# A scan-based decoder layer on one core: softplus without the inverse exponential, logarithms in place, and most Silus of z moved into the scan stage

## The chip, the cores and the metric

One core of one Trainium2 chip runs the whole program. The metric is the device time of one execution in microseconds, as a median over runs. All data is float32 in HBM.

## The reference, cut to what matters

Four sequences of 512 tokens of width 512 go through three residual blocks, each behind a layer norm. The change touches the first (a selective state-space block) and the order of work around the others: a SmoothQuant int8 feed-forward (its output is the "second residual") and a mixture of 16 experts, two per token, with a shared expert.

```python
xz = einsum(in_proj_weight, hidden)          # 512 -> 2048, halves x and z, 1024 channels each
x = silu(conv1d(x))                          # depthwise, 4 taps
dt, Bc, Cc = split(x_proj(x))                # 128, 16, 16
delta = softplus(dt_proj_weight @ dt + dt_proj_bias)
h = h * exp(delta * A) + (delta * u) * B     # 16 states per channel, one step per token
y = sum_n(h * C) + u * D
y = y * silu(z)
out = out_proj_weight @ y
```

Softplus is computed as relu(x) + ln(w) less a correction, with e = exp(-|x|) and w = 1 + e rounded. The correction makes good what the rounding of w lost: lost = (w - 1) - e, times 1/w.

## The kernel before, in words

**Tiling.** Channels lie in 8 blocks of 128 partitions, tokens (512) along the free axis. A batch's stage is 128 units (8 blocks times 16 states), p = 0 to 127 with a tail of 8. Per unit ScalarE makes exp(delta * A) (`decay`, line 942, into a ring of three PSUM banks), VectorE runs the scan over tokens (line 1277) and multiplies by C (`product`, line 1289; every eighth on GpSimd, line 718), GpSimd makes delta * u * B for two units at once (`chunk`, line 663, four slots; `du_block`, line 651, once per block) and adds every other pair of products (line 715), and TensorE sums over the states with identity matmuls into bank 7 (`nsum`, lines 1870 to 1881). `gated` (line 1297) then multiplies by silu(z).

**Interleaving.** While batch b is scanned, the experts of batch b - 1 run on the same engines: transposes and copy of the input (`x3`, line 956), router logits, routing on VectorE, eight "visits" of the shared expert (each `gate_up` on TensorE, `tanh_g` on ScalarE, `expert_gate` and `expert_up` on VectorE, `down` on TensorE), a scatter of rows by GpSimd's indirect DMA, then 23 visits of routed tiles. Everything is ordered by hand: each engine runs through p (GpSimd through k = p/2), and constants say at which p a step stands. A visit starts at `VISIT_AT[v]`, its tanh 3 units behind, the VectorE parts 4 and 5, the down matmuls 7. VectorE does scan(p), then product(p - 1), then the rest of p; ScalarE does decay(p + 2) first.

**The gap.** Between stages each engine has a list of its own (`between`, lines 1110, 1556 and 2099; GpSimd: `phase1`, line 688). It holds the projections x and z of the next batch, the convolution, both quantised matmuls of the feed-forward of the last batch, the norms, and softplus. Softplus for block m: ScalarE `relus` (Abs and Relu from PSUM), `exps` (line 895), VectorE `one_more` (w, line 1252) and `lost` (line 1258), ScalarE `lns` (line 909) and `inverses` (exp(-ln w), line 915), a multiply of lost by the inverse (GpSimd `softplus_lost`, line 636, for blocks 0 to 3; VectorE `softplus`, line 1266, for 4 to 7), and GpSimd's `softplus_sum` (line 629) and `softplus_less` (line 644) into delta. Blocks 4 to 7 use the rows of blocks 0 to 3 again, so they wait for them: `relus` and `one_more` of block m for the correction of block m - 4. The VectorE multiplies of blocks 4 to 7 stand at p = 1 of the stage, behind scans 0 and 1 and before product 0.

**Queues.** SP issues the weight loads (a ring of four for the projections), the broadcasts of B and C (four groups of four states; group 0 and 1 wait for the quantised matmuls, 2 and 3 for the second residual and for the weights behind z(7)), the experts' weights and rows. ScalarE issues the output store. The tables of ScalarE's functions are loaded by instructions that the compiler places where the function set changes.

**The first batch** has no gap: its softplus of blocks 1 to 7, its z and dt matmuls and their Silus are placed inside the stage (`EARLY_...` constants); block 0 is done ahead (`first`), with the multiply and the first chunk on VectorE. The last stage (b = 4) has experts alone.

The waits around the seam, which the steps follow:

```python
def product(c):                               # VectorE, line 1289
    if c == 0 and b > 0:
        ve.wait_ge(S["sp_err_ready"], NBLK * (b + 1))
def chunk(b, k):                              # GpSimd, line 663
    if k == 2 and b > 0:
        pool.wait_ge(S["sum_ready"], NBLK * (b + 1))
def integers(m, layer, side):                 # TensorE
    if side == 1:
        pe.wait_ge(S["wsc_ready"], r + 1)
def down(v):                                  # TensorE
    if v == 0:
        pe.wait_ge(S["route_done"], 2 * b)
```

## Time and profile before

| | |
|---|---|
| median of 3 runs | 1689.68 us (1688.85 to 1691.19) |
| the profiled execution: its span, first to last instruction | 1684.0 us |
| what lies between that span and the median | 5.7 us |
| instructions | 19335 |
| TensorE matmul, busy | 1428.3 us (85%) |
| VectorE, busy | 1344.6 us (80%) |
| GpSimd, busy | 1060.6 us (63%) |
| ScalarE, busy | 801.0 us (48%) |
| chain that ended last | PE 54%, DVE 17%, issue 12%, ACT 8%, POOL 7% |
| granted TensorE clock, mean | 0.938 of full speed |

The profile has no separate time for the profiled execution beside its span. PE is TensorE, DVE VectorE, ACT ScalarE, POOL GpSimd, PEld the weight loads, SP the queue that issues DMAs. Times in the rows are us from the span's start, unless marked ns. A timeline row merges like neighbours: "x4" is four instructions, and the duration is from the start of the first to the end of the last. The brackets give the idle time before the row and who ended it.

### The profile page before, as it was taken

Reading aid. Unit: us, or ns where it says so; the run is one execution under the profiler, and the core shown is the slowest. Engines: PE = TensorE matmul, PEld = TensorE weight load, DVE = VectorE, ACT = ScalarE, POOL = GpSimd, SP = SyncE. Lnnn points to the kernel's source line nnn. Section 1 sums busy time; section 2 is a strip of 40 time slices with the busy share of each in tenths; the row PEclk is TensorE's granted clock in tenths of the full one; section 3 lists DMA queues with packets and bytes.
Section 4 is the critical chain, followed back from the end, with each engine's and each line's share of the span. In section 5 each row is a group of like instructions: output and inputs, shape, how many; then the busy total and the mean of one; then the engine's idle time right before and its main releaser. Section 6 shows DMA issues by size and latency. Waiting matters only on the chain.

```text
span 1684.0 us, 19335 instructions
## 1 busy us (share of the span) xinstructions
PE 1428.3 (85%) x5368; PEld 809.6 (48%) x5376; DVE 1344.6 (80%) x2215; ACT 801.0 (48%) x1374; POOL 1060.6 (63%) x684
## 2 busy tenths in 40 slices
PE   7588679999599899999599899999599999836994
PEld 4233224444365565444265565444265665324783
DVE  4588999676899999786899999796899999784212
ACT  3666444246634565246634565245734565222141
POOL 0399898103999899402999899501999999522101
PEclk9899899999799999999799999999799999968997
DMA  3550001403446673613535674612534773700984
GB/s 119 220 187 25 1 0 38 135 28 116 192 138 184 208 237 123 212 38 105 228 118 188 207 234 142 212 38 102 231 113 153 233 235 130 250 25 20 350 334 140
DMA packets 94073, 252.13 MB, mean 150 GB/s; under 512 B 11024, under 2 KB 11152, under 8 KB 88848
## 3 DMA queue, kind: packets, MB, share of 16 engines
q1 hardware_dynamic: 86688, 229.93, 40.3%
q0 software_dynamic: 5120, 16.78, 3.1%
q10 hardware_dynamic: 2160, 4.19, 0.6%
q8 instruction: 44, 0.72, 0.2%
q14 instruction: 61, 0.50, 0.1%
HBM read 207.87 MB, written 42.99 MB: 149 GB/s over the span
## 4 chain that ended last, share of the span: by engine, by line
PE 54%; DVE 17%; issue 12%; ACT 8%; POOL 7%; DMA 1%; DVEq 0%; POOLq 0%; SPq 0%; ACTq 0%
PE bank L1946 10%; PE bank L1804 7%; DVE bank L1277 5%; PE bank L2072 5%; PE bank L1817 5%; PE bank L1876 4%; PE bank L1881 4%; POOL work L663 4%; PE bank L1975 3%; PE bank L1870 3%; PE bank L1967 2%; PE bank L1922 2%; DVE work L1289 2%; DVE pairs L1289 2%; PE bank L1845 2%
## 5 line engine op out<-in xcount | busy, mean ns | idle before, releaser
L663 POOL TENSOR_TENSOR work<-du,BB 128x1024 f32<-128x1024 f32 x255 | 598.8, 2357 | 5.2 <-DVE work L1553 4.4
L942 ACT ACTIVATE bank<-delta,A_sb 128x512 f32<-128x512 f32 x512 | 349.9, 690 | 460.7 <-DVE pairs L1289 246.2
L1277 DVE TENSOR_TENSOR_SCAN bank<-bank,work 128x512 f32<-128x512 f32 x432 | 522.6, 1219 | 7.8 <-POOL work L663 4.0
L1946 PEld LDWEIGHTS bank<-x3T,ew_up 128*128 128x128 f32 x1488 | 215.7, 193 | 72.5 <-issue 63.7
L1946 PE MATMUL bank<-x3T,ew_up 128*128 128x128 f32 (+1 forms) x1488 | 235.8, 304 | 5.2 <-issue 5.2
L1289 DVE TENSOR_TENSOR pairs<-bank,CB 128x512 f32<-128x512 f32 x240 | 161.0, 671 | 3.9 <-PE bank L1881 2.9
L608 POOL TENSOR_TENSOR col<-col,halfpow 128x4 f32<-128x4 f32 (+1 forms) x8 | 7.8, 973 | 208.9 <-DVE col L1429 208.9
L1876 PE MATMUL bank<-pairs,ident 128*128 128x512 f32 x160 | 91.9, 659 | 43.7 <-DVE pairs L1289 16.6
L1289 DVE TENSOR_TENSOR work<-bank,CB 128x512 f32<-128x512 f32 x192 | 128.3, 668 | 0.0
L1817 PE MATMUL bank<-xT,wst 128*128 128x512 f32 x256 | 118.8, 610 | 9.2 <-DVE ew_up L1266 7.4
L2072 PE MATMUL bank<-wst,zg 128*128 128x512 f32 x256 | 117.0, 593 | 0.9 <-DVE zg L1297 0.9
L1804 PE MATMUL bank<-xT,wst 128*128 128x512 f32 x256 | 114.4, 593 | 0.7 <-ACT xT L829 0.7
L1241 DVE SCALAR_TENSOR_TENSOR u<-etm,cw,u 128x512 f32<-128x512 f32 x96 | 72.2, 752 | 40.6 <-ACT u L849 38.3
L1304 DVE SCALAR_TENSOR_TENSOR etm<-etm,bank 128x128 f32<-128x128 f32 (+1 forms) x124 | 38.6, 311 | 80.5 <-ACT etm L995 80.5
L1876 PE MATMUL bank<-work,ident 128*128 128x512 f32 x160 | 83.5, 604 | 12.5 <-POOL work L718 10.2
L715 POOL TENSOR_TENSOR work<-work 128x512 f32<-128x512 f32 x48 | 60.7, 1266 | 45.5 <-DVE work L1289 45.3
L1975 PE MATMUL bank<-ew_dn,etm 128*128 128x512 f32 x138 | 73.2, 612 | 18.2 <-ACT x3T L1009 17.9
L718 POOL TENSOR_TENSOR work<-work,CB 128x512 f32<-128x512 f32 x64 | 81.3, 1271 | 10.9 <-DVE work L1277 10.9
L1881 PE MATMUL bank<-pairs,ident 128*128 128x512 f32 x160 | 86.7, 625 | 0.0
L848 ACT COPY etm<-bank 128x512 f32<-128x512 f32 x32 | 18.8, 587 | 140.7 <-PE bank L1804 140.7
L1277 DVE TENSOR_TENSOR_SCAN work<-bank,work 128x512 f32<-128x512 f32 x64 | 77.5, 1211 | 8.8 <-PE bank L1881 6.3
L1817 PEld LDWEIGHTS bank<-xT,wst 128*128 128x128 f32 x256 | 49.3, 195 | 72.6 <-issue 59.2
(259 smaller groups left out, 2493.4 us busy)
## 6 DMA issues: line engine op xcount, KB each, us to landing
ew_up<-in_exp_w SPq DMA_DIRECT2D x93, 512.0 KB, 3.7
ew_dn<-in_exp_w SPq DMA_DIRECT2D x93, 256.0 KB, 4.3
hm<-xs_dram SPq DMA_DIRECT2D x69, 256.0 KB, 4.6
ys_dram<-x3T SPq DMA_DIRECT2D x69, 256.0 KB, 4.6
wst<-in_w_in SPq DMA_DIRECT2D x64, 256.0 KB, 2.7
BB<-bc_dram SPq DMA_DIRECT2D x16, 1024.0 KB, 7.7
CB<-bc_dram SPq DMA_DIRECT2D x16, 1024.0 KB, 9.7
wst<-in_out_w SPq DMA_DIRECT2D x32, 256.0 KB, 3.0
```

The source lines that it names most:

```text
L663: nc.gpsimd.tensor_tensor(dBu[:, k % CHUNK_SLOTS, :, :], du[:, j % 2:j % 2 + 1, :].broadcast_to([P, 2, T]), BB[:, n0:n0 + 2, :], ALU.mult) ...
L718: nc.gpsimd.tensor_tensor(hi, hi, CB[:, (2 * m + 1) % NS, :], ALU.mult).then_inc(S["pool_prod"], 1)
L942: nc.scalar.activation(R[q % RING][:, :], delta[:, j, :], ACT.Exp, scale=A_sb[:, j, n:n + 1]).then_inc(S["da_ready"], 1)
L1277: V.tensor_tensor_scan(prod[c % (2 * PAIR_SLOTS)] if on_pool(q) else R[q % RING][:, :], R[q % RING][:, :], dBu[:, c // 2 % CHUNK_SLOTS, c ...
L1289: V.tensor_tensor(prod[c % (2 * PAIR_SLOTS)], R[q % RING][:, :], CB[:, n, :], ALU.mult).then_inc(S["prod_done"], 1)
L1804: ins = mm(ps[:, :], wst[:, slot, k * P:(k + 1) * P], xT[:, k, :], start=(k == 0), stop=(k == KD - 1))
L1817: ins = mm(z_bank(a, m)[:, :], wst[:, slot, k * P:(k + 1) * P], xT[:, k, :], start=(k == 0), stop=(k == KD - 1))
L1876: mm(Y[:, :], ident[:], prod[2 * (m % PAIR_SLOTS)], start=(m % (NS // 2) == 0), stop=False)
L1881: mm(Y[:, :], ident[:], prod[2 * (m % PAIR_SLOTS) + 1], start=False, stop=(m % (NS // 2) == NS // 2 - 1)).then_inc(S["nsum_done"], 1)
L1946: ins = mm(gu_bank(v)[:, part * n:(part + 1) * n], w[:, part * D + k * P:part * D + (k + 1) * P], rhs, start=(k == 0), stop=(k == KD - 1))
L1975: mm(down_ps[1][:, :], eT[:, v % 2, 0:P], w, start=True, stop=True).then_inc(S["down_done"], 1)
L2072: ins = mm(acc[t][:, :], zg[:, k, t * P:(t + 1) * P], wst[:, W_POS["o", m, k] % W_RING, :], start=(k == 0), stop=(k == NBLK - 1))
```

## The change

Softplus takes the correction without the factor 1/w: delta = relu + ln(w) - lost. The inverse exponentials, the multiplies and their semaphores go. The logarithm overwrites w, so in later batches it waits for `lost`; in the first batch `lost` overwrites w behind the logarithm. Blocks 4 to 7 have rows of their own: e in the slots of chunks 2 and 3, w in the rows of `x3T`. So chunks 2 and 3 wait for the corrections, and `x3` for the sums. The gap's lists are reordered on TensorE, ScalarE, VectorE and GpSimd. Raw z is copied out for blocks 2 to 7, and its Silu is taken in place at p = 20 and p = 60. In stages with scans x3, the logits, routing and the first seven visits stand later; the routed visits keep their places.

```diff
+    logits_copy: int
+    route: int
+    rank: int
+    place: int
+    first_down: int
+
+
+STAGE = Order(visits=tuple(6 + 15 * v // 4 for v in range(SHARED)) + tuple(38 + 3 * r for r in range(ROUTED)),
+              x3=3, logits=4, logits_copy=5, route=7, rank=11, place=12, first_down=14)
+LATE = Order(visits=tuple(4 + 4 * v for v in range(SHARED)) + tuple(38 + 3 * r for r in range(ROUTED)),
+             x3=0, logits=2, logits_copy=0, route=5, rank=9, place=10, first_down=12)
+RAW_Z = 2
+SILU_AT = {20: range(2, 5), 60: range(5, 8)}
 ROWS_BEFORE = 4
 ROWS_COPY_BEFORE = 2
 TANH_BEHIND = 3
 T1_BEHIND = 4
 T2_BEHIND = 5
 DOWN_BEHIND = 7
-FIRST_DOWN_AT = 12
 Y_COPY_BEHIND = 9
 FINISH_BEHIND = 9
...
-EARLY_INVERSE_AT = {1: 6, 2: 7, 3: 8, 4: 29, 5: 30, 6: 31, 7: 32}
-EARLY_LOST_AT = {1: 4, 2: 5, 3: 6, 4: 24, 5: 25, 6: 26, 7: 27}
-EARLY_ERROR_AT = {1: 8, 2: 9, 3: 10, 4: 31, 5: 32, 6: 33, 7: 34}
+EARLY_LOST_AT = {1: 6, 2: 7, 3: 8, 4: 29, 5: 30, 6: 31, 7: 32}
...
             if a == 0 and m > 0:
                 return dl_bank(a, m)[:, :]
-            return x2[:, (m + 3) % 4, :] if a == 0 else pairs[:, m % 4, :]
+            if a == 0:
+                return x2[:, (m + 3) % 4, :]
+            return pairs[:, m, :] if m < 4 else work[:, 4096 + (m - 4) * T:4096 + (m - 3) * T]
...
-            return ew_up[:, i // 2, i % 2 * D:(i % 2 + 1) * D] if a == 0 else late_pairs[:, m % 4, :]
+            if a > 0:
+                return late_pairs[:, m, :] if m < 4 else x3T[:, m - 4, :]
+            return ew_up[:, i // 2, i % 2 * D:(i % 2 + 1) * D]
 
...
             if a == 0:
                 return ew_dn[:, i, :] if i < DOWN_RING else x3T[:, 1, :]
-            return work[:, 4096 + m % 4 * T:4096 + (m % 4 + 1) * T]
+            return sp_w(a, m)
...
+            def softplus_less(a, m):
+
+                pool.wait_ge(S["sum_ready"], NBLK * a + m + 1)
                 pool.wait_ge(S["sp_lost"], NBLK * a + m + 1)
-                pool.wait_ge(S["sp_inv_ready"], NBLK * a + m + 1)
-                nc.gpsimd.tensor_tensor(sp_w(a, m), sp_e(a, m), sp_w(a, m), ALU.mult).then_inc(S["sp_err_ready"], 1)
-
-            def softplus_less(a, m):
-
-                pool.wait_ge(S["sum_ready"], NBLK * a + m + 1)
-                pool.wait_ge(S["sp_err_ready"], NBLK * a + m + 1)
                 if a == 0 and m == 1:
                     pool.wait_ge(S["delta_ready"], 1)
-                nc.gpsimd.tensor_tensor(delta[:, m, :], delta[:, m, :], sp_w(a, m), ALU.subtract
+                lost = sp_w(0, m) if a == 0 else sp_e(a, m)
+                nc.gpsimd.tensor_tensor(delta[:, m, :], delta[:, m, :], lost, ALU.subtract
                                         ).then_inc(S["delta_ready"], 1)
...
-                if k == 2 and b > 0:
-                    pool.wait_ge(S["sum_ready"], NBLK * (b + 1))
+                if k in (2, 3) and b > 0:
+                    pool.wait_ge(S["delta_ready"], NBLK * b + 2 * k + 2)
...
                 if a is not None:
-                    for i in range(4):
+                    for i in range(2):
                         softplus_sum(a, i)
-                    for i in range(4):
-                        softplus_lost(a, i)
-                    softplus_less(a, 0)
+                        softplus_less(a, i)
                     du_block(a, 0)
                     chunk(a, 0)
-                    for i in range(1, 4):
+                    for i in range(2, 4):
+                        softplus_sum(a, i)
                         softplus_less(a, i)
                 if m is not None:
                     norm(2 * m + 1)
                 if a is not None:
-                    for i in range(4, 8):
-                        softplus_sum(a, i)
+                    chunk(a, 1)
...
-                        if k > 0:
+                        if k == 2 and b > 0:
+                            for i in range(4, 8):
+                                softplus_sum(b, i)
+                            for i in range(4, 6):
+                                softplus_less(b, i)
+                        if k > (1 if b > 0 else 0):
                             chunk(b, k)
-                        if k == 1 and b > 0:
-                            for i in range(4, 8):
+                        if k == 2 and b > 0:
+                            for i in range(6, 8):
                                 softplus_less(b, i)
...
-                nc.scalar.activation(zg[:, m, :], z_bank(a, m)[:, :], ACT.Silu).then_inc(S["z_ready"], 1)
+                nc.scalar.activation(zg[:, m, :], z_bank(a, m)[:, :], ACT.Silu if a == 0 or m < RAW_Z else ACT.Identity
+                                     ).then_inc(S["z_ready"], 1)
+
+            def z_silu(a, m):
+                sc.wait_ge(S["z_ready"], NBLK * a + m + 1)
+                nc.scalar.activation(zg[:, m, :], zg[:, m, :], ACT.Silu).then_inc(S["z_silu"], 1)
...
-                    if m >= 4:
-                        sc.wait_ge(S["sp_err_ready"], NBLK * a + m - 3)
+                    if a == 0 and m >= 4:
+                        sc.wait_ge(S["sp_lost"], m - 3)
...
-                    if m >= 4:
-                        sc.wait_ge(S["sum_ready"], NBLK * a + m - 3)
+                    if a > 0:
+                        sc.wait_ge(S["sp_lost"], NBLK * a + m + 1)
+                    elif m >= 4:
+                        sc.wait_ge(S["sum_ready"], m - 3)
...
+                        if scan:
+                            sc.wait_ge(S["sum_ready"], NBLK * (b + 1))
...
-                if experts:
-                    for i in range(KD if scan else KD // 2):
-                        x3(i)
-                    logits_copy()
                 for p in range(UNITS + TAIL):
                     if scan and RING <= p + 2 < UNITS:
                         decay(b, p + 2)
+                    if experts:
+                        if p == at.x3:
+                            for i in range(KD if scan else KD // 2):
+                                x3(i)
+                        if p == at.logits_copy:
+                            logits_copy()
+                    if scan and b > 0:
+                        for m in SILU_AT.get(p, ()):
+                            z_silu(b, m)
...
                 if m > 0:
                     store(m - 1)
+                exps(a, range(0, 1))
                 z(a, 2)
                 relus(a, range(1, 2))
+                exps(a, range(1, 2))
                 z(a, 3)
                 relus(a, range(2, 3))
+                exps(a, range(2, 3))
+                magic_rows(m, 1, 0)
                 z(a, 4)
                 relus(a, range(3, 4))
-                exps(a, range(4))
-                magic_rows(m, 1, 0)
+                exps(a, range(3, 4))
                 magic_rows(m, 1, 1)
                 lns(a, range(4))
                 weight_scales(m, 1)
-                inverses(a, range(4))
                 z(a, 5)
+                relus(a, range(4, 5))
                 z(a, 6)
-                relus(a, range(4, 8))
+                relus(a, range(5, 8))
+                exps(a, range(4, 8))
                 z(a, 7)
-                exps(a, range(4, 8))
                 for c in range(RING):
                     decay(a, c)
+                row_norm(m, 2 * m + 1)
                 lns(a, range(4, 8))
-                row_norm(m, 2 * m + 1)
-                inverses(a, range(4, 8))
 
             def last(m):
 
...
             def one_more(a, m):
 
                 ve.wait_ge(S["sp_exp"], NBLK * a + m + 1)
-                if m >= 4:
-                    ve.wait_ge(S["delta_ready"], NBLK * a + m - 3)
+                if m == 4:
+                    if a == 1:
+                        ve.wait_ge(S["xs_zeroed"], 16 * ROUTED)
+                    else:
+                        ve.wait_ge(S["gu_done"], VISITS * (a - 1))
+                        for i in range(2):
+                            ve.wait_ge(ys_out[i], 16 * ring_uses(a - 1, i))
                 V.tensor_scalar(sp_w(a, m), sp_e(a, m), 1.0, None, ALU.add).then_inc(S["sp_w_ready"], 1)
 
             def lost(a, m):
 
                 e, w = sp_e(a, m), sp_w(a, m)
                 ve.wait_ge(S["sp_w_ready"], NBLK * a + m + 1)
-                V.scalar_tensor_tensor(out=e, in0=w, scalar=1.0, in1=e,
+                if a == 0:
+                    ve.wait_ge(S["sp_ln_ready"], m + 1)
+                V.scalar_tensor_tensor(out=w if a == 0 else e, in0=w, scalar=1.0, in1=e,
                                        op0=ALU.subtract, op1=ALU.subtract).then_inc(S["sp_lost"], 1)
-
-            def softplus(a, m):
-
...
             def scan_stage(b, scan, experts):
 
@@ -1283,9 +1303,7 @@
                     ve.wait_ge(bcast[n // 4], 32 * (b + 1))
                     wait(ve, "nsum_done", PAIRS * b + c // 2 - PAIR_SLOTS + 1)
                     if c == 0 and b > 0:
-                        ve.wait_ge(S["sp_err_ready"], NBLK * (b + 1))
-                    if 4 <= c < 8 and b > 0:
-                        ve.wait_ge(S["delta_ready"], NBLK * b + c + 1)
...
                         ve.wait_ge(S["z_ready"], j + 1)
+                    elif j >= RAW_Z:
...
                     if scan and p < UNITS:
                         scan_unit(p)
-                    if scan and p == 1 and b > 0:
-                        for i in range(4, 8):
-                            softplus(b, i)
                     if scan and b == 0:
...
                 q1.diag(0)
                 q1.diag(1)
+                for i in range(2):
+                    one_more(a, i)
+                    lost(a, i)
                 q1.scale(0)
                 q1.maxima(0)
                 q1.scale(1)
                 q1.maxima(1)
                 q1.weight_diag()
-                for i in range(4):
+                for i in range(2, 4):
                     one_more(a, i)
                 q1.integers(0)
-                for i in range(4):
+                for i in range(2, 4):
                     lost(a, i)
                 q1.integers(1)
...
                 for i in range(4, 8):
                     one_more(a, i)
-                for i in range(4, 8):
                     lost(a, i)
...
+                        pe.wait_ge(S["sp_lost"], m + 1)
                 elif m < 2:
...
@@ -1979,16 +1997,16 @@
                     norm_transposes(2 * b - 1, xn, acc, "xn_ready", "tr_done")
                 for p in range(UNITS + TAIL):
                     if experts:
-                        if p == LOGITS_AT:
+                        if p == at.logits:
                             logits()
...
                 dl(a, 0)
                 z(a, 2)
                 dl(a, 1)
+                gated_rows(m)
                 z(a, 3)
-                gated_rows(m)
                 dl(a, 2)
+                diag_rows(m, 1, 0)
+                diag_rows(m, 1, 1)
                 z(a, 4)
                 dl(a, 3)
-                diag_rows(m, 1, 0)
-                diag_rows(m, 1, 1)
                 z(a, 5)
                 dl(a, 4)
+                scale_rows(m, 1)
                 z(a, 6)
-                dl(a, 5)
-                scale_rows(m, 1)
                 integers(m, 1, 0)
                 integers(m, 1, 1)
+                dl(a, 5)
                 linear(m, 1)
-                z(a, 7)
                 dl(a, 6)
                 dl(a, 7)
+                z(a, 7)
```

In the rest of the diff the constants `ROUTE_AT` and the like become fields of `at` (the tables above), with the same offsets between the steps.

## Rows read from the trace of the kernel before

**Rows 1.** Busy us by stretch: PE, PEld, DVE, ACT, POOL; clock; DMA

```profile
444.00:469.00 25.00, 19.31 (x77) 12.22 (x76) 24.00 (x58) 9.13 (x17) 25.00 (x15) 0.93 0.07 22
469.00:501.00 32.00, 32.00 (x108) 20.28 (x107) 31.77 (x46) 12.38 (x21) 30.06 (x23) 1.00 0.44 151
...
815.00:828.00 13.00, 8.73 (x25) 4.20 (x25) 10.30 (x9) 9.29 (x16) 12.31 (x8) 0.61 0.55 217
```

**Rows 2.** Chain of waits: start, us, what

```profile
435.48 1.28 ACT L915
437.50 2.87 DVE work L1266
```

**Rows 3.** Groups by line: VectorE, whole run; ScalarE, 395 to 445

```profile
L1266 DVE TENSOR_TENSOR work<-pairs,work 128x512 f32<-128x512 f32 x12 | 20.4, 1756 | 7.7 <-ACT work L915 7.7
...
L915 ACT ACT_TABLE_LOAD x2 | 2.6, 1283 | 0.0
```

**Rows 4.** Timeline of VectorE, second batch's gap: start, us, what

```profile
392.77 1.29 DVE L1425 TENSOR_REDUCE col<-bank 128x1 f32<-128x512 f32 x2 [5.56 <-PE bank L2054]
...
405.45 1.42 DVE L1252 TENSOR_SCALAR work<-pairs 128x512 f32<-128x512 f32 x4
...
421.96 1.27 DVE L1212 TENSOR_SCALAR mv<-mv 128x4 f32<-128x4 f32 x1
425.80 4.48 DVE L1252 TENSOR_SCALAR work<-pairs 128x512 f32<-128x512 f32 x4 [2.57 <-ACT pairs L895]
...
432.61 2.33 DVE L1277 TENSOR_TENSOR_SCAN bank<-bank,work 128x512 f32<-128x512 f32 x2
...
444.43 0.69 DVE L1289 TENSOR_TENSOR pairs<-bank,CB 128x512 f32<-128x512 f32 x1
```

**Rows 5.** Timeline of ScalarE in the same gap

```profile
338.90 1.14 ACT L854 ACTIVATE u<-u 128x512 f32<-128x512 f32 x2
...
410.30 0.56 ACT L1074 COPY CB<-bank 128x512 f32<-128x512 f32 x1
...
432.54 2.92 ACT L1069 ACTIVATE xn<-x,row_shift,rstd 128x512 f32<-128x512 f32 x4
```

**Rows 6.** Timeline of TensorE, same gap and stage front

```profile
388.26 3.60 PE L1817 MATMUL bank<-xT,wst 128*128 128x512 f32 x8
...
412.72 3.10 PE L2046 MATMUL bank<-CB 128*128 128x512 bf16 x7 [1.19 <-DVE CB L1489]
...
439.48 5.30 PE L1887 MATMUL bank<-x3T,gatew 128*17 128x512 f32 x8 [2.35 <-ACT x3T L956]
...
468.02 1.96 PE L1967 MATMUL bank<-ew_dn,etm 128*128 128x512 f32 x4 [1.68 <-DVE posi L1744]
```

**Rows 7.** Timeline of GpSimd, same gap and stage front

```profile
408.91 6.81 POOL L629 TENSOR_TENSOR delta<-delta,work 128x512 f32<-128x512 f32 x4 [13.67 <-ACT work L909]
...
423.29 2.34 POOL L663 TENSOR_TENSOR work<-du,BB 128x1024 f32<-128x1024 f32 x1
...
452.45 2.35 POOL L663 TENSOR_TENSOR work<-du,BB 128x1024 f32<-128x1024 f32 x1
```

**Rows 8.** Timeline of VectorE, second batch's stage

```profile
457.38 1.22 DVE L1277 TENSOR_TENSOR_SCAN bank<-bank,work 128x512 f32<-128x512 f32 x1
...
471.89 1.23 DVE L1277 TENSOR_TENSOR_SCAN bank<-bank,work 128x512 f32<-128x512 f32 x1
...
484.00 0.41 DVE L1304 SCALAR_TENSOR_TENSOR etm<-etm,bank 128x256 f32<-128x256 f32 x1
...
562.72 2.46 DVE L1202 BATCH_NORM_STATS2 st<-xn 128x6 f32<-128x512 f32 x4
```

**Rows 9.** Timelines of ScalarE and VectorE, first stage

```profile
99.00 0.69 ACT L942 ACTIVATE bank<-delta,A_sb 128x512 f32<-128x512 f32 x1 [1.76 <-DVE work L1289]
...
105.38 1.30 ACT L942 ACTIVATE bank<-delta,A_sb 128x512 f32<-128x512 f32 x2 [1.01 <-DVE work L1289]
...
103.54 1.22 DVE L1277 TENSOR_TENSOR_SCAN work<-bank,work 128x512 f32<-128x512 f32 x1 [4.63 <-PE bank L1881]
```

76 lines of the change are left out of this document (31 added, 45 removed).

## The prediction

> **What bounds the kernel now.** I read the busy shares by stretch first, then the chain of waits through the second batch's gap and stage, then each engine's timeline there. A batch is a "gap" (projections, quantised matmuls, norms; about 310 to 444 us for the second batch) and a stage of 128 scans. Inside the stage three engines are nearly full: VectorE is busy 31.77 of 32 us and TensorE all 32 [rows 1]. So a stage has little slack to swallow a late engine, and an earlier start of all three is kept. At the seam it is otherwise. The first product of the stage stands at 444.43 us although two scans are done by 434.9, because it waits for the softplus correction [rows 4]. The chain of waits there runs through ScalarE's reload of the Exp table and VectorE's correction multiply [rows 2], then GpSimd's chunks of dt·B·u. The seams of batches 3 and 4 have the same order of waits, so one gap is worked out and used three times.
>
> **What the change removes.** For each later batch: eight ScalarE exponentials with two table loads (1.28 us each), four VectorE and four GpSimd multiplies. The VectorE ones last 1756 ns each on average, the loads 1283 ns [rows 3]. The gap now has seven loads (two each for exponential, logarithm and inverse, one for Silu of z). With z stored raw from block 2 on, the Exp set stays in, and I count Exp, Ln, Exp, Ln and one Exp at the first decay in the stage: five. The stage gets four new ones.
>
> **The gap, step by step.** (1) TensorE does its gated transposes before z(3) instead of after it. One z is 8 matmuls, 3.43 us apart [rows 6], so VectorE's column maxima start at about 389.4 us, not 392.77 [rows 4]. (2) VectorE puts two one-mores and two losts (0.34 and 0.60 us each, 1.9 us) where it waited 1.82 us for TensorE. Scale and maxima then run as before, 3.3 us earlier. (3) The rest of the quantised down projection hangs on ScalarE's copy of the weight scales, now at 410.30 us behind Exp and Ln blocks [rows 5]. With exponentials interleaved I get: magic rows to 404.8, table load, four logarithms to 408.3, copy to 408.9. The integer transposes follow, linear starts near 410.4 instead of 412.72 [rows 6], and the variance is out near 420.7, not 423.2 [rows 4]. (4) GpSimd: first sum at 406.75 instead of 408.91 [rows 7], and that first sum was stretched by VectorE's two-input operations to 3.1 us. Sums and corrections 0 and 1 (four of 1.25), du (1.25) and chunk 0 (2.34 [rows 7]) end at 415.4; sums and corrections 2 and 3 at 420.3; norm 2.4 us to 423.1; chunk 1 to 425.5. Product 0 asks only for the fourth correction, 420.3. (5) ScalarE: relus 4 to 7, exponentials to 419.6, z(7), three decays to 422.1, row norm 423.2 to 426.1 (2.92 us, it stood at 432.54 [rows 5]), table load, logarithms 4 to 7 by 429.6. (6) GpSimd's k=2 now holds sums 4 to 7 and corrections 4, 5 ahead of chunk 2: from 428.0 six operations to 435.5, chunk 2 to 437.9, two corrections, chunk 3 to 442.6, one pair, chunk 4 to 446.2. Chunk 4 now ends at 454.7 (452.45 plus 2.3 [rows 7]). GpSimd gains **8.5 us**.
>
> **Added waits.** ScalarE's x3 copies wait for the four late sums, which end at 433.0. Queued behind them are the decays from scan 6 on; scan 4 cannot start before chunk 2 at 437.9, so I cost this at nothing. If it lost that cover, decay 6 would be late and scan 6 with it. Chunks 2 and 3 wait for corrections 4 to 7, which is in the sum. SP's queue: the last broadcasts wait for z(7) and the residual; z(7) ends at 418.2 against 419.9, so they go out no later and land before chunk 4. Separate rows for blocks 4 to 7 take away waits only. The first VectorE one-mores of blocks 4 to 7 took 4.48 us for four beside GpSimd, against 1.42 us for four without [rows 4]; even at 7 us for the eight operations scans 0 to 2 fit before decay 3, which needs its reload and comes at 431.5.
>
> **The front of the stage.** Logits: x3 copies end at 436.1, TensorE needs 5.30 us as before [rows 6], the copy to the router waits behind decay 7 (442.0), and the first gate_up starts at 443.1 against 445.8, only 2.7 us sooner. TensorE then has pauses, and the first down projection waits for the routing. VectorE reaches scan 8 at 446.5 instead of 457.38 [rows 8], but has 1.4 us of routing still to do. I get routing done at 461.6, so down(0) moves from 468.02 [rows 6] to 461.7, with gate_up(2,0) of 1.7 us already behind it: TensorE gains **8.2 us**. VectorE stands **9.7 us** earlier at scan 14, now at 471.89 [rows 8]: about 462.2. From here to scan 32 the three are packed.
>
> **Silus in the stage.** ScalarE at p=20: a decay 0.6, load 1.28, three Silus at 0.57 (a pair from SBUF took 1.14 [rows 5]), load 1.28, then tanh of visit 3, done 5.4 us after product 19. VectorE wants that tanh at p=21, after scan, product and gated: 2.3 us after product 19. A decay ring of three hides the decays but not the tanh: a stall of **3.1 us**. The expert gate before stands right behind a product with no wait [rows 8], so nothing hides it on VectorE. At p=60 the head's statistics keep VectorE busy 2.46 us plus aggregation [rows 8], together 3.2 us of cover: no stall in batches 2 and 3. Batch 4 has no head there, and I get up to 2.3 us, of which I take 1.5. Bounds for one group: above, the spacing of the decays around four Silus in the first stage, 99.00 to 105.38 us [rows 9], 6.4 us; below, zero, since VectorE waited for TensorE there anyway. I take 3.1, worked out from single durations, because three Silus from SBUF are less than four and TensorE has no z to catch up with here.
>
> In the timeline the load of 1283 ns [rows 3] is followed by its activation at once. The Trainium skill, "ScalarE: Activation LUTs", section "What ACT_TABLE_LOAD costs", gives 2.66 us for a switch with its drain, and its rules say to finish one set before the next, which speaks against splitting the Silus. By that price a group would hold ScalarE 2.8 us longer and the sum would be some 8 us worse over three stages, about 1673; the rows here do not show the drain.
>
> VectorE: 9.7 - 3.1 = 6.6 us; GpSimd 8.5; TensorE 8.2. The least counts: **6.5 us** for batches 2 and 3, **5** for batch 4.
>
> **The first batch.** Before its first scan a load, the inverse and the multiply (1.28, 0.63 and 0.69 us) lie in line; now lost (0.7) follows the logarithm, and less waits for the sum, 1.2 us long: 1.4 us sooner. In the stage seven multiplies of 0.6 us go from VectorE and seven exponentials from ScalarE. z(1) waited for the corrected block; now it waits for lost, some 6 us sooner, so the 4.63 us wait of scan 15 on TensorE [rows 9] shrinks to about 1. Silus of z at p=14 then come bare and give 2 us back. Net 4.3 by scan 18, another 2.4 by scan 28 from the losts that leave a packed stretch; **6.5 us**, between 3 (only VectorE's multiplies) and 8.
>
> **Sum.** 6.5 + 6.5 + 6.5 + 5 = 24.5 us. The profiled execution spans 1684.0 us, giving 1659.5; the median of the runs, 1689.68, lies 5.7 above that span, and I keep this distance: **1665 us**. The last, scanless stage has its own order table with the old places, worth nothing.
>
> **Rivals.** (a) *TensorE starts the stage.* Only x3 and the logits count, 2.7 us per stage, with 6.5 from the first batch: 14.6 us, 1675. For it: TensorE is full from down(0) on. The granted clock was 0.61 in 815 to 828 [rows 1], and TensorE will now idle twice there, so gate_up could run slow. Against: it has pauses before down(0). (b) *The Silu stall is hidden*, because TensorE, not VectorE, is last at p=21: 8.2 to 8.5 per stage and 6.5, 31.5 us, 1658. (c) *Gains spent again*: (a) with the p=20 stall and the one at p=60 in batch 4: 3 x (2.7 - 3.1) - 2.3 + 6.5 = 3, so 1686.7, no measurable change. (d) *Slower*: ScalarE becomes what the stage waits for. If each of two groups costs the full 6.4 us of rows 9, a stage loses 12.8 against 8.5 won: +4.3 each, +12.9; with the x3 wait holding decay 6 another 1 us per stage and 6.5 won in front, +9.4, 1699. It decides once two groups cost more than 8.5 + 2.2 = 10.7 us. Against: the ring of three decays covers 5.6 us. (e) *The loads aren't saved*: the decays need Exp anyway, and I counted only two fewer in the gap; this moves (3) and (5) by 1.3 us each, inside the range.
>
> **How the numbers follow.** A measurement here can tell about 0.2%, 3.4 us, from no change. Chances: the forecast (1659 to 1671) 0.50, (a) 0.17, (b) 0.19, (c) 0.06, (d) 0.08. Faster 0.87, same 0.05, slower 0.08. The range takes in (a), (b) and both ends of the first batch's term: 1654 to 1681.
>
> **What would show it.** The first product of the second stage near 427, scan 4 near 438, scan 8 near 446.5, and scan 32 only 6 to 7 us ahead of before. Five table loads at the seam, four in each later stage. VectorE waiting about 3 us for tanh at p=21 and for nothing at p=60 until batch 4. In the first stage scan 15 near 97. Wrong would be: scan 4 not set by chunk 2; decays late after x3; gate_up at half clock with a VectorE wait at the rank; or equal gains at scan 14 and scan 32.

## The result and the profile after

The changed kernel takes **1665.61 us** in the median of 4 runs (1661.16 to 1668.67); the kernel before took 1689.26 (1687.18 to 1691.19) on the same chip. The ratio is 0.9855, with a 95% interval from 0.9836 to 0.9874: a gain of about 1.5%, clear of the noise, and the forecast of 1665 is met. A second comparison on another occasion gave 1666.80 against 1689.06, ratio 0.9843 (0.9811 to 0.9875).

The profiled execution spans 1659.4 us, 24.6 less than the 1684.0 of before. From the page of the profile: busy time of each engine, then the costliest group of GpSimd and the costliest of VectorE (busy us, mean ns, idle before and its releaser).

```profile
PE 1424.9 (86%) x5368; PEld 809.5 (49%) x5376; DVE 1322.9 (80%) x2195; ACT 799.8 (48%) x1366; POOL 1033.7 (62%) x672
...
L672 POOL TENSOR_TENSOR work<-du,BB 128x1024 f32<-128x1024 f32 x255 | 598.9, 2357 | 5.4 <-DVE work L1568 3.5
...
L1297 DVE TENSOR_TENSOR_SCAN bank<-bank,work 128x512 f32<-128x512 f32 x432 | 522.0, 1220 | 27.7 <-POOL work L672 21.2
```

The chunks and the scans are what they were; what is new is that the scans wait 21.2 us in all for GpSimd's chunks, where they waited 4.0 before. Where that happens is seen in the second batch. All times of this batch lie 4.6 us earlier than they otherwise would, because the first batch had already given 4.6. So a time of the forecast, which was told on the clock of before, is to be compared with a row here plus 4.6. The timeline of VectorE (start, us, operation, what the idle time before it ended on):

```profile
385.07 1.29 DVE L1441 TENSOR_REDUCE col<-bank 128x1 f32<-128x512 f32 x2 [2.13 <-PE bank L2072]
...
414.61 0.47 DVE L1232 TENSOR_SCALAR mv<-mv 128x4 f32<-128x4 f32 x1
...
424.63 0.67 DVE L1307 TENSOR_TENSOR pairs<-bank,CB 128x512 f32<-128x512 f32 x1
...
433.52 1.23 DVE L1297 TENSOR_TENSOR_SCAN bank<-bank,work 128x512 f32<-128x512 f32 x1 [4.67 <-POOL work L672]
...
442.31 2.33 DVE L1297 TENSOR_TENSOR_SCAN bank<-bank,work 128x512 f32<-128x512 f32 x2
...
458.67 1.22 DVE L1297 TENSOR_TENSOR_SCAN bank<-bank,work 128x512 f32<-128x512 f32 x1
...
475.17 0.42 DVE L1324 SCALAR_TENSOR_TENSOR etm<-etm,bank 128x256 f32<-128x256 f32 x1 [1.70 <-ACT etm L1011]
```

The maxima wait 2.13 us for TensorE instead of 5.56, the variance is out at 415.1, the first product stands at 424.63 instead of 444.43 [rows 4], and scan 4 waits for the chunk as forecast. Scans 8 and 14 start at 442.31 and 458.67, against 457.38 and 471.89 [rows 8]. ScalarE, gap and first group of Silus:

```profile
403.79 0.56 ACT L1093 COPY CB<-bank 128x512 f32<-128x512 f32 x1
...
418.57 2.94 ACT L1088 ACTIVATE xn<-x,row_shift,rstd 128x512 f32<-128x512 f32 x4 [1.57 <-POOL row_shift L634]
421.52 1.28 ACT L928 ACT_TABLE_LOAD   x1
422.82 2.19 ACT L928 ACTIVATE x3T<-x3T 128x512 f32<-128x512 f32 x4
...
471.91 1.28 ACT L875 ACT_TABLE_LOAD   x1
473.20 1.67 ACT L875 ACTIVATE zg<-zg 128x512 f32<-128x512 f32 x3
474.78 0.36 ACT L1011 ACTIVATE etm<-bank 128x256 f32<-128x256 f32 x1
475.16 1.28 ACT L954 ACT_TABLE_LOAD   x1
```

GpSimd: the first sum, chunks 1, 2 and 4, and the first indirect transfer that scatters the routed rows:

```profile
402.40 1.27 POOL L643 TENSOR_TENSOR delta<-delta,work 128x512 f32<-128x512 f32 x1 [14.86 <-ACT work L928]
...
418.49 2.36 POOL L672 TENSOR_TENSOR work<-du,BB 128x1024 f32<-128x1024 f32 x1
...
431.08 2.34 POOL L672 TENSOR_TENSOR work<-du,BB 128x1024 f32<-128x1024 f32 x1 [0.17 <-POOL delta L653]
...
439.55 2.36 POOL L672 TENSOR_TENSOR work<-du,BB 128x1024 f32<-128x1024 f32 x1
...
458.73 1.23 POOL L755 DMA_INDIRECT xs_dram<-xn,posi  x1 [2.09 <-DVE posi L1761]
```

Chunk 4 ends at 441.9 instead of 454.8 [rows 7]: 12.9 us, of which 8.3 belong to this seam. But then GpSimd stands idle for 2.09 us until the router's positions are there. TensorE:

```profile
406.04 1.67 PE L2064 MATMUL bank<-CB 128*128 128x512 bf16 x7
...
430.15 6.41 PE L1905 MATMUL bank<-x3T,gatew 128*17 128x512 f32 x8 [6.98 <-ACT x3T L972]
...
438.69 5.41 PE L1964 MATMUL bank<-x3T,ew_up 128*128 128x256 f32 x16
...
458.57 1.95 PE L1985 MATMUL bank<-ew_dn,etm 128*128 128x512 f32 x4 [0.61 <-DVE posi L1761]
```

The linear product no longer waits for the integers (1.67 us instead of 3.10), the logits took 6.41 us instead of 5.30, the first 16 gate_up matmuls 5.41 us instead of 3.72, and the first down projection stands at 458.57, against 468.02 [rows 6]. The busy time over the same work, scans 0 to 7 of the second batch, before and then after, and of the 32 us that follow 447 (busy us of PE, PEld, DVE, ACT, POOL; granted clock; DMA):

```profile
432.61:457.38 24.77, 17.76 (x52) 9.66 (x53) 21.49 (x37) 14.04 (x26) 24.07 (x15) 0.72 0.35 131
```

```profile
422.38:442.31 19.93, 11.17 (x26) 4.71 (x25) 13.78 (x19) 10.80 (x18) 18.45 (x13) 0.59 0.46 184
447.00:479.00 32.00, 31.39 (x123) 21.10 (x122) 29.52 (x55) 14.34 (x22) 29.02 (x21) 1.00 0.34 115
```

Now TensorE and VectorE have more room in the front of the stage, and TensorE's clock is lower there: 0.59 of 2.4 GHz, a mixture of its two levels (1.2 and 2.4 GHz), where over the same scans it was 0.72 before. The third batch has 0.67 against 0.73; only the fourth is not lower, 0.76 against 0.73. In the first stage the two rows of VectorE that answer to [rows 9]:

```profile
97.34 1.22 DVE L1297 TENSOR_TENSOR_SCAN work<-bank,work 128x512 f32<-128x512 f32 x1
...
103.48 1.23 DVE L1297 TENSOR_TENSOR_SCAN bank<-bank,work 128x512 f32<-128x512 f32 x1 [3.19 <-ACT bank L954]
```

### The profile page after: what moved, and what is told of

It reads as the page before. It is cut to its first block, busy times and chain, and to the rows that moved or that the text cites. A ratio compares the mean times of both kernels' runs of the same rounds, so it can differ in the third digit from the quotient of the medians.

```text
span 1659.4 us, 19244 instructions
## 1 busy us (share of the span) xinstructions
PE 1424.9 (86%) x5368; PEld 809.5 (49%) x5376; DVE 1322.9 (80%) x2195; ACT 799.8 (48%) x1366; POOL 1033.7 (62%) x672
## 4 chain that ended last, share of the span: by engine, by line
PE 49%; DVE 16%; issue 15%; POOL 14%; ACT 4%; DMA 1%; DVEq 0%; POOLq 0%; SPq 0%; ACTq 0%
PE bank L1964 10%; PE bank L1821 7%; POOL work L672 5%; DVE bank L1297 5%; PE bank L2090 5%; PE bank L1894 4%; PE bank L1899 4%; PE bank L1993 3%; PE bank L1888 2%; PE bank L1834 2%; PE bank L1985 2%; DVE pairs L1307 2%; PE bank L1940 2%; POOL delta L643 2%; DVE work L1307 2%
## 5 line engine op out<-in xcount | busy, mean ns | idle before, releaser
L1297 DVE TENSOR_TENSOR_SCAN bank<-bank,work 128x512 f32<-128x512 f32 x432 | 522.0, 1220 | 27.7 <-POOL work L672 21.2
L1964 PE MATMUL bank<-x3T,ew_up 128*128 128x128 f32 (+1 forms) x1488 | 239.8, 306 | 2.2 <-issue 2.2
L1894 PE MATMUL bank<-work,ident 128*128 128x512 f32 x160 | 84.7, 611 | 15.1 <-POOL work L725 11.7
L1899 PE MATMUL bank<-work,ident 128*128 128x512 f32 x160 | 83.5, 604 | 0.0
```

The source lines that it names most:

```text
L1297: V.tensor_tensor_scan(prod[c % (2 * PAIR_SLOTS)] if on_pool(q) else R[q % RING][:, :], R[q % RING][:, :], dBu[:, c // 2 % CHUNK_SLOTS, c ...
L1894: mm(Y[:, :], ident[:], prod[2 * (m % PAIR_SLOTS)], start=(m % (NS // 2) == 0), stop=False)
L1899: mm(Y[:, :], ident[:], prod[2 * (m % PAIR_SLOTS) + 1], start=False, stop=(m % (NS // 2) == NS // 2 - 1)).then_inc(S["nsum_done"], 1)
L1964: ins = mm(gu_bank(v)[:, part * n:(part + 1) * n], w[:, part * D + k * P:part * D + (k + 1) * P], rhs, start=(k == 0), stop=(k == KD - 1))
```

## The experiments

Levels of whole executions move by some microseconds, but the distances of scans within a stage agree closely. So the main measure is the **gain at scan k**: how much earlier that scan starts than in the profile of before, less the gain of the last scan of the previous stage. The table is worked out from the starts of the 512 scans in each trace. "scatter" is the same gain for GpSimd's first indirect transfer. Scans, scatter and end are of the third stage; ends 2 and 4 are those of the second and the fourth.

```
kernel                         median us  ratio [95%]               scan4 scan24 scatter scan32  end | end2 end4
changed (first profile)        1665.61    0.9855 [0.9836, 0.9874]     9.9    5.8     5.8    5.9  7.1 |  8.6  3.0
changed again (e12)            1666.80    0.9843 [0.9811, 0.9875]    10.1    6.0     6.0    6.1  7.2 |  8.7  3.1
e1 Silus at unit 0             1668.32    0.9860 [0.9823, 0.9897]    11.3    8.4     6.6    6.7  6.2 |  5.7  4.1
e2 Silus at unit 3             1673.63    0.9891 [0.9847, 0.9936]    11.3    6.7     4.9    5.1  3.3 |  3.5  4.5
e3 first group at unit 22      1667.94    0.9852 [0.9810, 0.9893]     9.9    7.6     5.8    5.8  7.1 |  8.5  3.0
e4 TensorE's order of before   1681.21    0.9956 [0.9938, 0.9974]     5.0    2.0     2.0    2.1  3.3 |  4.5 -0.7
e5 visits of before            1666.89    0.9868 [0.9848, 0.9888]    10.2    6.6     5.7    5.6  7.4 |  7.8  3.1
e6 first batch only            1683.82    0.9963 [0.9949, 0.9976]     0.0    0.0     0.0   -0.1  0.1 | -1.0  0.2
e7 factor only, rows shared    1695.25    1.0021 [1.0005, 1.0038]    -3.5   -5.6    -2.8   -5.0 -5.2 | -6.5 -5.8
e8 Silus in gap, lists before  1678.26    0.9921 [0.9903, 0.9939]     6.6    5.4     3.6    3.7  3.2 | -0.6  3.2
e9 as e8, TensorE before too   1683.88    0.9956 [0.9936, 0.9976]     3.2    2.0     0.2    0.3 -0.2 | -0.1 -0.2
```

**The parts, taken away one by one.** e7 makes only the first edit: the inverse exponential and the multiply go, everywhere, and the rows of blocks 0 to 3 stay shared with blocks 4 to 7. So each relu of blocks 4 to 7 must wait until GpSimd has applied the correction whose row it overwrites.

```diff
                     if m >= 4:
-                        sc.wait_ge(S["sp_err_ready"], NBLK * a + m - 3)
+                        sc.wait_ge(S["sp_lost"] if a == 0 else S["delta_ready"], NBLK * a + m - 3)
...
                 weight_scales(m, 1)
-                inverses(a, range(4))
```

> The kernel before with the factor 1/w dropped in all batches (inverse exponentials and multiplies gone), but blocks 4 to 7 still in the rows of blocks 0 to 3 and every list in its old order; relus 4 to 7 now wait for the corrections 0 to 3 that read e. My theory (shared rows give back what the dropped work saves): first batch -4.6 us; at the later seams GpSimd saves 5 us of multiplies and VectorE its multiplies, but relus 4 to 7 wait until about 416 to 420: 2 to 5 us per seam, 1669 to 1679 in all. Rival (the dropped work is the whole gain): 1666. Rival (the reordering is the whole gain of the later seams): 1684.

The expectation was missed: instead of gaining 10 to 20 us it was **slower** than before, 1.0021 (1.0005 to 1.0038). The profiled execution ends the later stages 6.5, 5.2 and 5.8 us behind, but it took 1702.71 us against a median of 1695.25, so these ends overstate the loss. Of the 6.5 us in the second stage only 2.0 are there at scan 64. The other 4.5 come by scan 72, around one VectorE operation that took 7.24 us, where the others of its kind take about 0.5 and no other kernel shows such a one; its cause stays open:

```profile
577.07 7.24 DVE L1214 SCALAR_TENSOR_TENSOR shift<-mv,rstd 128x4 f32<-128x4 f32 x1
```

What the seam alone costs is read at scan 4: 2.2, 3.5 and 3.1 us. ScalarE's timeline of e7, and then VectorE's:

```profile
416.31 0.69 ACT L879 ACTIVATE pairs<-bank,dtb 128x512 f32<-128x512 f32 x1 [3.77 <-POOL delta L642]
...
421.31 0.69 ACT L879 ACTIVATE pairs<-bank,dtb 128x512 f32<-128x512 f32 x1 [3.74 <-POOL delta L642]
```

```profile
446.08 0.69 DVE L1282 TENSOR_TENSOR pairs<-bank,CB 128x512 f32<-128x512 f32 x1 [10.97 <-POOL delta L642]
```

Two waits of 3.8 us each for GpSimd, the second because the correction stands behind chunk 0, and the first product then waits 10.97 us until the last correction has freed its row. So in e7 the waits for shared rows cost more than the dropped arithmetic saves. e9 gives blocks 4 to 7 their own rows, with the logarithms in place, GpSimd's new order and the new places in the stage, but leaves the lists of the other engines in the gap as before:

```diff
-            return x2[:, (m + 3) % 4, :] if a == 0 else pairs[:, m % 4, :]
+            if a == 0:
+                return x2[:, (m + 3) % 4, :]
+            return pairs[:, m, :] if m < 4 else work[:, 4096 + (m - 4) * T:4096 + (m - 3) * T]
```

> The gap's lists of TensorE, ScalarE and VectorE as before (less the inverses), all Silus in the gap; kept are the dropped factor, logarithms in place, own rows for blocks 4 to 7, GpSimd's new order and the places in the stage. It differs from the kernel that only dropped the factor by the rows, GpSimd's order and those places. If sharing the rows was what made that kernel slower (ScalarE's relus 4 and 5 waited 3.8 and 3.7 us for GpSimd's corrections 0 and 1), these waits are gone and scan 4 of the second stage comes at least 2 us ahead of before, against 2 to 3.5 us behind it there, and the time is 1674 to 1682. Rival: the rows hardly matter and the gain of the change sits in the reordered lists: scan 4 within 1 us of before, 1684 or more.

Of the expectation the place came true (scan 4 is 2.8 to 3.2 us ahead) and the time did not: 1683.88 is the rival's 1684, for nothing of it is left at the end of a stage (-0.1, -0.2, -0.2). The step from e7 to e9 holds four edits at once, so the share of the rows alone is not shown, only that the waits of relus 4 and 5 for a row are gone. ScalarE of e9:

```profile
413.33 0.69 ACT L900 ACTIVATE work<-bank,dtb 128x512 f32<-128x512 f32 x1
...
421.64 0.69 ACT L900 ACTIVATE work<-bank,dtb 128x512 f32<-128x512 f32 x1 [5.87 <-PE bank L1868]
```

Relu 4 goes without a wait, but relu 6, and 7 behind it, now wait 5.87 us for TensorE, whose list still holds them back. e8 is e9 with TensorE's new order; e4 is the changed kernel with TensorE's old one, whose edit begins:

```diff
                 dl(a, 1)
+                z(a, 3)
                 gated_rows(m)
-                z(a, 3)
                 dl(a, 2)
+                z(a, 4)
+                dl(a, 3)
                 diag_rows(m, 1, 0)
                 diag_rows(m, 1, 1)
-                z(a, 4)
-                dl(a, 3)
...
```

> The changed kernel with all Silus of z back in the gap and ScalarE's and VectorE's gap lists as before (less the inverses): exponentials 0 to 3 in one block behind z(4), one-mores and losts 0 to 3 behind the weight diagonal. TensorE's and GpSimd's lists as changed. My theory (raw z pays by taking the table switches out of the gap; the weight-scale copy comes 1 to 2 us later and the exponentials 4 to 7 behind one more load): each later seam 2 to 4 us worse, the stage 1.7 us better (no wait for tanh) and batch 4 another 2.4 us better: about 0 to +4 us. Rival (the Silus in the stage are pure cost): -5 to -7 us.

> TensorE's list of the gap as it was before the change, everything else changed. My theory (z(3) ahead of the gated transposes delays VectorE's maxima by 3.4 us, and variance, row norm, logarithms 4 to 7 and GpSimd's chunks hang on them): scan 4 to 8 of each later stage 3 us later, +8 to +10 us in all. Rival (the softplus chain on ScalarE and GpSimd sets the seam alone and the reorder only keeps TensorE tidy): under 3 us in all.

TensorE's order is worth 3.4 us by the end of the third stage between e9 and e8, and 3.8 between e4 and the changed kernel (7.1 against 3.3). e4 lost more than expected: 5 us at scan 4 instead of 3, and 11.6 us over the three stages instead of 8 to 10. ScalarE's and VectorE's lists with z stored raw are worth 3.9 in the third stage (7.1 against e8's 3.2), but 9.2 in the second and nothing in the fourth (3.0 against 3.2); 2.5 and 1.7 us of the first two come only between scans 64 and 72, where TensorE's clock differs (last section). So e8 takes some 12 us more than the changed kernel where at most 4 were expected. In VectorE's timeline of e4 the column maxima are again held by the z in front of the transposes:

```profile
391.31 1.29 DVE L1441 TENSOR_REDUCE col<-bank 128x1 f32<-128x512 f32 x2 [5.57 <-PE bank L2072]
```

From this the ladder of the third stage: factor alone -5.2 (overstated, see above), own rows, logarithms in place, GpSimd's order and the new places to -0.2, TensorE's order to +3.2, the other lists and raw z to +7.1.

**The first batch alone** (e6: before, with the changed softplus in batch 0 only).

```diff
-                            if p == EARLY_INVERSE_AT[m]:
-                                inverses(0, (m,))
...
                 lns(0, (0,))
-                inverses(0, (0,))
```

> The kernel before with the changed softplus in the first batch alone (blocks 0 to 7 of batch 0: no inverse exponential, no multiply, lost behind the logarithm). My theory: all of the 4.6 us that scan 48 and later of the first stage gained come from this, and nothing of it is lost later: 1684.5 us against 1689.3. Rival (what the first stage gives is taken back at the first seam, which waits for weights or loads): 1687 or more.

1683.82, ratio 0.9963 (0.9949 to 0.9976), which takes in the 4.8 us expected. The profile gives 4.1 us by the end of the first stage, 3.6 of them after its first scan, and the three later stages lose 0.7 of it (-1.0, 0.1, 0.2).

**Where the visits stand** (e5: those of before, 4 + 4v instead of 6 + 15v/4).

```diff
-STAGE = Order(visits=tuple(6 + 15 * v // 4 for v in range(SHARED)) + tuple(38 + 3 * r for r in range(ROUTED)),
+STAGE = Order(visits=tuple(4 + 4 * v for v in range(SHARED)) + tuple(38 + 3 * r for r in range(ROUTED)),
```

> The eight shared visits of stages with scans back at p = 4, 8, ..., 32 instead of 6, 9, 13, ..., 32; the rest of the stage's table as changed. My theory (TensorE has pauses before the first down projection and reaches visit 7 at the same p either way): within 2 us of the changed kernel, 1663 to 1668. Rival (the two units of delay keep gate_up from standing in front of the first sums over states while the logits are late): 1 to 3 us slower per stage, 1669 to 1675.

1666.89, as expected; the ends are 7.8, 7.4, 3.1 against 8.6, 7.1, 3.0: under 1 us, in both directions.

**The Silus.** Three kernels move them; each changes the one line of their places.

```diff
-SILU_AT = {20: range(2, 5), 60: range(5, 8)}
+SILU_AT = {0: range(2, 8)}
```

(e1; e2 has unit 3 for all six, e3 has unit 22 for the first group.)

> All six Silus of raw z at p=0 of the stage, behind the logarithms and ahead of decay 3, against the changed kernel (1661 to 1669 us). My theory (the Silus of p=20 cost each later stage the 1.7 us that VectorE waited for tanh, and those of p=60 the last of them 2.4 us): both waits go, 7.5 us, but six Silus (0.57 us each) and one load (1.28 us) hold decay 3 from 426.3 to about 431, so scan 3 and with it product 2, decay 5 and the x3 copies come 4 us later; if the logits then set the front, 3 us of each stage are lost again: net 0 to -2 us. Rival (the front is set by GpSimd's chunk 2 at 433.4, so decay 3 has cover): the whole 7.5 us, about 1658.

> All six Silus at p=3, behind the x3 copies, where ScalarE stood idle 3.8 us before decay 6. My theory: load, six Silus, load take 6.0 us from 431.5, decay 6 is ready at 438.2 and scan 6 started at 438.48, decay 7 at 438.8 is still ahead of scan 7 at 440.2; the logits copy moves by 1.1 us. The tanh wait of p=21 and the wait at p=60 of batch 4 are gone: -5 to -7.5 us against the changed kernel. Rival (the logits chain sets the front): about -4. Rival (the waits at p=21 and p=60 are absorbed anyway, because TensorE is full): 0.

> The first group of Silus at p=22 in place of p=20, where no tanh stands behind it before p=24; the group of p=60 stays. My theory (the tanh, not the decays, is what VectorE waited for; the ring of three covers the decays): the 1.7 us wait at p=21 goes in three stages and none takes its place, scan 32 about 1.7 us earlier per stage, -3 to -5 us in all. Rival (ScalarE's hold itself costs, wherever it stands): a wait for decay 25 of 1 to 2 us appears and the time is the same.

e1 came out as its theory said, at no measurable difference (0.9860 against 0.9855 and 0.9843). e2 missed: 5 to 7.5 us less were expected, 4 less or none by its rivals, and the stages end 7.4 us later in all. For e3 the rival holds: a wait for decay 25, and the same time. VectorE's timelines of e3 and of e1:

```profile
484.83 1.23 DVE L1297 TENSOR_TENSOR_SCAN bank<-bank,work 128x512 f32<-128x512 f32 x1 [2.36 <-ACT bank L954]
```

```profile
500.80 1.23 DVE L1297 TENSOR_TENSOR_SCAN bank<-bank,work 128x512 f32<-128x512 f32 x1 [1.26 <-POOL work L672]
```

In e3 the 1.70 us wait for tanh is gone; scan 25 waits 2.36 us for its decay instead, and that alone gives the gain at scan 32: 8.6 us ahead at scan 24, less 2.36, plus the 0.63 us that scan 32 waited before and here does not. In e1 neither wait exists, and in this second stage VectorE is 7.4 us ahead at scan 24 (6.8 in the changed kernel), only to wait 1.26 us for GpSimd's chunk at scan 32. The changed kernel waits there too, so its wait for tanh decided nothing; VectorE is only 0.67 us early, though (0.49 and 0.51 in the next two stages):

```profile
496.00 1.23 DVE L1297 TENSOR_TENSOR_SCAN bank<-bank,work 128x512 f32<-128x512 f32 x1 [0.67 <-POOL work L672]
```

That chunk follows from GpSimd's **first scatter**: in the table, the columns scatter and scan 32 agree within 0.2 us in every kernel but e7 (and in the other two stages too, but for e7 and for e5 in the second, where they differ by 1.2). The row from GpSimd's timeline of e1:

```profile
463.55 1.23 POOL L755 DMA_INDIRECT xs_dram<-xn,posi  x1 [3.25 <-DVE posi L1761]
```

GpSimd idles 3.25 us there for the positions (2.09 in the changed kernel; 0.65 before, where GpSimd was late itself), and from then on it is full.

The positions in turn follow from TensorE's first 16 gate_up matmuls, which stand in its list ahead of the matmuls of the ranking. In all stages of all kernels with the changed places the scatter starts 14.6 to 15.2 us after the end of these 16 (20.7 to 20.9 in the kernel before). How long they take differs: 3.72 us, 5.41 (the changed kernel, in each stage) or 6.5 to 6.7. e8 has two of these in one program, in its second and third stage. TensorE and then GpSimd:

```profile
446.67 6.65 PE L1957 MATMUL bank<-x3T,ew_up 128*128 128x256 f32 x16
...
829.40 3.72 PE L1957 MATMUL bank<-x3T,ew_up 128*128 128x256 f32 x16
```

```profile
467.95 1.23 POOL L755 DMA_INDIRECT xs_dram<-xn,posi  x1 [3.51 <-DVE posi L1754]
...
848.30 1.08 POOL L755 DMA_INDIRECT xs_dram<-xn,posi  x1 [0.90 <-DVE posi L1754]
```

Over the first row the granted clock is 0.55, over the second 1.00. The scatter starts 38.57 us after the first scan of the stage in the one (429.38) and 36.00 in the other (812.30), so the low clock costs 2.6 us of the front, and the gain at scan 32 is 0.7 against 3.7. In the changed kernel the 16 take 1.7 us longer than at the full clock, which by the distances above keeps the scatter back by an estimated 1.1 to 1.7 us. e2, with the Silus between the copies for the logits and their result, starts its first gate_up 1.1 us later than the changed kernel and takes 6.5 to 6.6 us for it; it has the least gain at the scatter of the three in the second and third stages.

**The second group in the last stage with scans.** e10 and e11 have the first group at unit 22 and, in that stage only, the second at unit 34 or 90 instead of 60.

```diff
+SILU_LAST = {22: range(2, 5), 34: range(5, 8)}
...
-                        for m in SILU_AT.get(p, ()):
+                        for m in (SILU_LAST if b == B - 1 else SILU_AT).get(p, ()):
```

> First Silu group at unit 22 in all three stages, and in the last stage with scans the second group at unit 34 instead of 60. Theory: the second group costs batch 4 its 2.5 us at unit 60 because VectorE has no head statistics there; between units 32 and 40 ScalarE is busy only 39 per cent of the time and TensorE is last, so there it costs at most 1 us: the last stage gains 4.3 to 5.3 us by its end instead of 3.0, and the time is 1 to 2.5 us below the changed kernel's, hardly to be told by the times but plain from the positions of the scans. Rival: a group costs about 2.5 us wherever it stands without cover: 3.0 or less at the end. The gain of unit 22 over 20 is gone again by scan 32, as in the earlier run.

> As the kernel with unit 34, but the second group of the last stage with scans at unit 90, behind the routed visits' first ones and before block 5's gate at unit 101; ScalarE is busy 65 per cent there, and VectorE and TensorE are both full. Theory: with TensorE the later of the two, up to 1 us is lost, and the stage gains 4.3 or more. Rival: as at unit 60, the decays come late behind load, Silus, load and the row copies, and 2 to 3 us go: 3 or less at the end.

> The changed kernel as it is, beside the three below on the same chip. Expected: 1664 to 1668 us, and from the second stage on the same positions of its scans as in its first profile, within 0.3 us: at scan 24 and scan 32 ahead of before by 6.8 and 6.8 (stage 2), 5.8 and 5.9 (3), 5.7 and 5.8 (4), at the end by 8.6, 7.1 and 3.0.

e12 repeats the positions of the first profile within 0.2 us. e10 and e11 take 1667.29 (ratio 0.9842, 0.9809 to 0.9875) and 1667.10 (0.9840, 0.9807 to 0.9872) beside its 1666.80: no difference. The rival of both holds: the fourth stage ends 3.0 and 2.5 us ahead, against 3.1. The three waits, in VectorE's timelines of the changed kernel, of e10 and of e11:

```profile
1308.31 1.22 DVE L1297 TENSOR_TENSOR_SCAN work<-bank,work 128x512 f32<-128x512 f32 x1 [2.38 <-ACT bank L954]
```

```profile
1260.84 0.42 DVE L1325 SCALAR_TENSOR_TENSOR etm<-etm,bank 128x256 f32<-128x256 f32 x1 [2.61 <-ACT etm L1012]
```

```profile
1366.68 1.23 DVE L1298 TENSOR_TENSOR_SCAN bank<-bank,work 128x512 f32<-128x512 f32 x1 [2.67 <-ACT bank L955]
```

A group of three makes VectorE wait 2.4 to 2.7 us at each of the three places tried behind scan 32 in this stage. The loss moves, it does not vanish, and none of the kernels beats the changed one.

## Why the prediction was right, point by point

**The sum.** Forecast: 6.5 for the first batch, 6.5, 6.5 and 5 for the others, 24.5. Measured in the profile: 1.1 before the first scan, 3.6 from there to the end of the first stage, then 8.6, 7.1 and 3.0, and 1.4 after the last scan: the 24.6 of the spans, but for rounding. The agreement is better than the terms. The first batch (4.6) was put too high by 1.9, the last by 2.0, the second and third too low by 2.1 and 0.6. The second profile of the changed kernel spans 1665.5, with the same stages (3.6, 8.7, 7.2, 3.1) but -2.1 before the first scan and -2.0 after the last. So only the 22.2 to 22.6 us of the stages are shown by both profiles; what the change does before the first scan is open. The medians differ by 23.7 and 22.3.

**The gap, steps (1) to (6)**, as forecast and as measured plus 4.6:

```
step                               forecast   measured + 4.6
column maxima                         389.4   389.7
copy of the weight scales ends        408.9   409.0
linear starts                         410.4   410.6
variance out                          420.7   419.7
first sum                            406.75   407.0 (1.27 us, no longer 3.1)
chunk 1 ends                          425.5   425.5
row norm starts                       423.2   423.2
logarithms 4 to 7 end                 429.6   429.6
chunk 2 ends, scan 4 starts           437.9   438.0, 438.1
chunk 4 ends                          446.2   446.5
first gate_up                         443.1   443.3
```

All are from single durations of before, and each is within 1 us. The five table loads at the seam and four in each later stage are there. One number was inconsistent: the first product "near 427" is at 429.2, because VectorE's own eight operations took 7.4 us from 415.0 to 422.4 and two scans follow, as my 7 us would have given; it cost nothing, since scan 4 waits for chunk 2 anyway. The waits of ScalarE's x3 copies for the late sums cost nothing either, as said.

**The front of the stage: the step that was missing.** I took GpSimd's 8.5 us at chunk 4 (measured 8.3) as kept, and let VectorE's wait for tanh bring the stage down to 6.5. The wait was 1.70 us and not 3.1, since the tanh went ahead of the reload, and it decided nothing: the changed kernel still waits 0.67 us for GpSimd at scan 32, behind the group. What limits the front of the stage is the router's chain: copies, logits, gate_up, rank, positions, then GpSimd's scatter in line before the chunks. It gained 6.8, 5.8 and 5.7 us. The forecast had the chain in it for TensorE only (down(0) at 461.7; measured 463.2), with gate_up at its old speed, and it never asked what else is queued behind the positions. That the minimum came to 6.5 all the same is luck of size, not of reasoning, and twice over: VectorE's own term was 9.7 less 3.1, and it measures 8.6 at scan 14 less 1.7, which is 6.9. Two errors cancel there, and VectorE comes out 0.67 us short of being the limit itself. Of TensorE's term, 8.2 (its parts, 6.3 and 1.7, make 8.0), the 1.7 for the gate_up taken ahead holds, and the rest was 4.9 (468.02 less 458.57, less 4.6): 6.6 in all.

**The group at unit 60** was forecast free in batches 2 and 3 and at 1.5 (up to 2.3) in batch 4. It cost 2.5 in batch 4, the mis-sized term. In batches 2 and 3 it was not free but gave 2.5 and 1.7 us back (below), and that is the unexpected part of those two terms: without it they would have ended at 6.1 and 5.4, the gain at scan 64.

**The first batch.** The wait of scan 15 for TensorE is gone, where about 1 us of it was forecast to stay (scan 15 at 97.34, "near 97"). By scan 15, 5.1 us are won within the stage; but the bare Silus of z then cost 3.3, not 2: the 3.19 us wait for ScalarE. From scan 18 to 32 another 1.8 came, forecast 2.4.

**Rivals.** (a), TensorE starting the stage: its slow clock did appear (the first 16 gate_up matmuls took 5.41 us at 438.69, and the windows above show 0.59) and takes its part in the router's chain, but the gain of 5.7 to 6.8 at scan 32 is more than its 2.7. (b), the stall hidden: it is hidden, but by GpSimd's chunks and not by TensorE, and its 8.2 to 8.5 are wrong, since what hides the stall stands at 5.8 to 6.8. (c) and (d): a group costs 2.4 to 2.7 us, far under the 5.4 that (d) needs of each. (e): the loads were saved as counted. The load was followed at once by its activation (471.91 plus 1.28, then 473.20), so the 2.66 us of the Trainium skill, "ScalarE: Activation LUTs", section "What ACT_TABLE_LOAD costs", are not met here; by an estimate from them the time would have been near 1673.

## What to carry to other kernels

Before an edit that removes work, ask what else its buffers and semaphores were ordering: here removing the arithmetic alone made the kernel slower, and it paid in the later stages only once the rows were separate and each engine's list was put in the order in which the others need its results. When an early start is to be kept through a packed stage, follow not only the engines' loads but each queued item that waits for a long chain (here one scatter that waits for the router); the item with the least gain limits the stage, and a second one can stand close behind it. And compare positions within a stage rather than whole times when the question is a microsecond or two, over the same work and not over the same length, and look for a single odd operation before a difference is given a cause.
